# Attention and gated feed-forward on one core: feed-forward steps between the attention's groups, the causal mask of the maxima on VectorE, silu by tanh

## The chip, the cores and the metric

The kernel runs on one core of a Trainium2 chip. The metric is device time in microseconds for one execution, the median of several runs. TensorE (PE) multiplies matrices into PSUM, VectorE (DVE) and ScalarE (ACT) read PSUM, GpSimd (POOL) works on SBUF alone, and SyncE (SP) issues the DMAs. Each engine works off its own instructions in order; semaphores hold one engine until another has done a step.

## What is computed

The input x is 8 x 512 x 128 (batch B, tokens T, channels C), with 16 heads of 8 channels, and all is fp32:

```python
qkv = x @ w_qkv                       # 128 -> 3*128
att = einsum('bhtd,bhsd->bhts', q, k) / sqrt(8)
att = softmax(where(causal, att, -inf))
x = layernorm(x + einsum('bhts,bhsd->bhtd', att, v))
gate, up = x @ (w_gate/127).T, x @ (w_up/127).T      # 128 -> 384
x = layernorm(x + (silu(gate) * up) @ (w_down/127).T)
```

## The kernel before

**Batches and groups.** A batch has 16 heads in four groups of four heads, so there are 32 groups, each named G in the program. `group` on TensorE (line 392 and on) is one step of a software pipeline with five slots. In the step of group G it computes in each slot a part of the scores of G (`scores`, transposed: keys on partitions), two of the ten banks of maxima of group G + 2 (`maxima`), and in slots 1, 2 and 4 the products of the exponentials with V for group G - 1 (`values`). Slot 1 also turns the row maxima of group G + 1 to rows (`turn_negmax`), and in every second group slot 2 turns the attention's output back (`turn_out`). Numbered from a batch's first step, n = 0 also projects V of the next batch and turns x (slot 3), and n = 1 projects Q and K of the batch after the next (slot 3).

**Maxima.** The softmax needs each row's maximum over the causal keys ahead of the scores. `maxima` computes untransposed scores: banks k = 0 to 3 hold 512 keys of one head, banks 4 to 7 hold 384 and 128, banks 8 and 9 hold 256 and 256. Two more bf16 matmuls a bank (`tri`, line 369) add -3e38 to what lies above the diagonal. VectorE's `reduce_group` (line 679) reduces each bank to its maximum by a `tensor_reduce` (line 693). Then POOL splits the maxima in two parts, TensorE turns them, ACT copies them and a DMA puts them into `qx` as two rows more, which the scores' matmuls subtract.

**PSUM.** Eight banks: two pairs (`st_ps`) that scores and projections take in turns, three single banks (`mx_ps`) and one for the values. Place p of a group's sequence uses `mx_ps[p % 3]`. The maxima have the places below, so k = 3 and k = 4 share a bank, the turned maxima lie between k = 4 and k = 5, and the turned output comes before k = 6:

```python
MX_PLACE = (0, 1, 2, 3, 6, 7, 8, 9, 10, 11)
NM_PLACE = 4
OT_PLACE = 5
```

TensorE waits on `mx_reduced` until the bank's reader is done, and with k = 6 of every second group until `attn_made`, which VectorE raises after `normalise` (line 697).

**ACT and POOL.** ACT computes one exponential of 128 x 1024 for each slot (`exp_slot`, line 589) and copies. POOL clears what lies above the diagonal in the exponentials (`clear_diagonal`, line 874), splits the maxima, and adds the attention to x (line 881).

**Feed-forward.** It stands behind all attention, in a loop over the batches (`ffn` on each engine). VectorE makes the statistics (lines 756 and 760), POOL the inverse deviation by a power (line 909) and x1 (line 920), TensorE turns x1, ACT and VectorE split it in a high and a low part, 12 matmuls make gate and up in three pieces of 128 hidden channels (lines 524 and 527), ACT applies silu (line 658), VectorE multiplies (line 791), 24 matmuls go down (line 536), VectorE adds the residual (line 779) and makes new statistics, POOL normalises into `yo` (line 931) and SP stores it.

## Time and profile before

| | us |
|---|---|
| median of three runs | 431.03 (425.5 to 435.24) |
| the profiled execution | 426.48 |
| its span, first to last instruction | 424.8 |
| TensorE busy | 378.4 (89%) |
| VectorE busy | 279.6 (66%) |
| ACT busy | 215.1 (51%) |
| POOL busy | 169.1 (40%) |

The share of busy time is an average over stages. A line of the profile names the engine, the line of the kernel, the operation with output and input, how many were merged, and in brackets how long the engine was idle before and whom it waited for. Ends of matmuls are modelled, and pipelined matmuls overlap, so the distance between two starts says more than a duration. "PEclk" is the granted TensorE clock as a share of 2.4 GHz; 0.5 is the lower level, 1.2 GHz.

### The profile page before, as it was taken

The page shows a single profiled execution, that of the slowest core. Times are in us where ns is not written, and L with a number is a line of the kernel's source. Part 1 is how long each engine was busy: PE and PEld are TensorE (multiplying, and loading weights), DVE is VectorE, ACT ScalarE, POOL GpSimd, SP SyncE. Part 2 cuts the span into 40 slices and gives each one's busy share as a digit, 9 for nine tenths or more (in the row PEclk, how much of TensorE's full clock was granted, in tenths as well). Part 3 has the DMA queues.
Part 4 walks back from the last instruction along what each step waited for, and adds up shares of the span by engine and source line. Part 5 has one row for each costly group of instructions (what it writes and reads, how often), then busy time and mean ns, then how long its engine had stood idle before and what let it go on. Part 6 is the DMA issues. An engine that isn't in the chain of part 4 may idle for free.

```text
span 424.8 us, 8778 instructions
## 1 busy us (share of the span) xinstructions
PE 378.4 (89%) x3285; PEld 223.6 (53%) x3288; DVE 279.6 (66%) x580; ACT 215.1 (51%) x277; POOL 169.1 (40%) x346
## 2 busy tenths in 40 slices
PE   5599979999999999999999999999999886888872
PEld 3344544555555555555555545555555344766761
DVE  6368663745677677768777786777777414777661
ACT  2203553544566666667566675656666564223220
POOL 8701221311423433242243324223432446678844
PEclk9869895955999999999999999999999898999998
DMA  5740562431226425331651443055200000010101
GB/s 167 264 138 3 198 188 66 174 124 41 69 86 217 140 61 200 102 103 56 228 144 55 166 137 102 29 205 164 61 2 5 14 18 0 16 35 25 52 25 49
DMA packets 33897, 41.72 MB, mean 98 GB/s; under 512 B 3136, under 2 KB 17472, under 8 KB 33856
## 3 DMA queue, kind: packets, MB, share of 16 engines
q1 hardware_dynamic: 33856, 41.17, 30.3%
q8 instruction: 26, 0.43, 0.4%
q14 instruction: 15, 0.12, 0.1%
HBM read 21.76 MB, written 18.87 MB: 96 GB/s over the span
## 4 chain that ended last, share of the span: by engine, by line
PE 59%; DVE 21%; POOL 7%; issue 4%; DMA 4%; ACT 3%; SPq 1%; POOLq 0%; DVEq 0%
PE psum L379 16%; PE psum L360 14%; DVE nm L693 13%; PE psum L349 9%; PE psum L325 5%; PE psum L369 4%; POOL x L920 3%; DMA scr_k<-parts 2%; PE psum L389 2%; PE psum L315 2%; PE psum L337 2%; POOL rstd L909 2%; DVE stats L756 2%; PE psum L331 2%; DVE attn L704 1%
## 5 line engine op out<-in xcount | busy, mean ns | idle before, releaser
L693 DVE TENSOR_REDUCE nm<-psum 128x1 f32<-128x512 f32 (+2 forms) x320 | 201.7, 684 | 88.5 <-PE psum L369 88.3
L589 ACT ACTIVATE pt<-psum 128x1024 f32<-128x1024 f32 x160 | 159.6, 1024 | 98.9 <-PE psum L349 98.4
L874 POOL TENSOR_SCALAR_AFFINE_SELECT pt<-pt 128x512 f32<-128x512 f32 x128 | 78.9, 635 | 156.2 <-ACT pt L589 155.9
L360 PE MATMUL psum<-kx,qx 33*128 33x384 f32 (+3 forms) x512 | 101.9, 362 | 15.7 <-DVE nm L693 5.5
L379 PE MATMUL psum<-pt,vx 128*32 128x512 f32 (+3 forms) x1024 | 95.4, 471 | 1.0 <-ACT pt L589 1.0
L349 PE MATMUL psum<-qx,kx 35*128 35x384 f32 (+3 forms) x512 | 84.0, 381 | 2.6 <-DMA qx<-nm_T 1.7
L349 PEld LDWEIGHTS psum<-qx,kx 35*128 35x128 f32 x512 | 44.6, 195 | 68.8 <-issue 51.3
L360 PEld LDWEIGHTS psum<-kx,qx 33*128 33x128 f32 x512 | 60.3, 197 | 31.6 <-DVE nm L693 18.0
L369 PE MATMUL psum<-tri 64*128 64x128 bf16 (+1 forms) x640 | 61.7, 219 | 0.0
L369 PEld LDWEIGHTS psum<-tri 64*128 64x128 bf16 x640 | 29.7, 100 | 23.6 <-issue 20.4
L379 PEld LDWEIGHTS psum<-pt,vx 128*32 128x32 f32 x1024 | 24.3, 111 | 20.4 <-issue 5.4
L658 ACT ACTIVATE sg<-psum 128x512 f32<-128x512 f32 x24 | 14.3, 597 | 28.7 <-PE psum L527 28.7
L881 POOL TENSOR_TENSOR res<-res,attn 128x512 f32<-128x512 f32 x8 | 10.2, 1271 | 41.5 <-DVE attn L704 41.5
L536 PE MATMUL psum<-wT,pt 128*128 128x128 f32 x192 | 22.9, 276 | 1.5 <-DVE pt L791 1.5
L536 PEld LDWEIGHTS psum<-wT,pt 128*128 128x128 f32 x192 | 22.5, 192 | 2.8 <-DVE pt L791 2.3
L527 PE MATMUL psum<-x_lo,wT 128*128 128x512 f32 x48 | 20.5, 426 | 2.0 <-DVE x_lo L772 2.0
L524 PE MATMUL psum<-x_hi,wT 128*128 128x512 f32 x48 | 21.4, 445 | 0.7 <-ACT x_hi L650 0.7
L325 PE MATMUL psum<-xT,wqkv 128*128 128x512 f32 x32 | 20.5, 774 | 0.8 <-ACT xT L568 0.8
L596 ACT ACTIVATE nm_T<-psum 32x128 f32<-32x128 f32 x32 | 8.5, 266 | 22.3 <-PE psum L337 19.6
L862 POOL TENSOR_SCALAR nm_parts<-nm 128x16 fp32r<-128x16 f32 x32 | 6.6, 206 | 28.9 <-DVE nm L695 28.8
L791 DVE TENSOR_TENSOR pt<-psum,sg 128x512 f32<-128x512 f32 x24 | 16.0, 670 | 2.9 <-ACT sg L658 2.0
L672 DVE TENSOR_TENSOR parts<-psum,parts 128x512 fp32r<-128x512 f32 x16 | 11.1, 691 | 9.1 <-ACT parts L575 9.0
(63 smaller groups left out, 289.7 us busy)
## 6 DMA issues: line engine op xcount, KB each, us to landing
scr_q<-parts SPq DMA_DIRECT2D x16, 512.0 KB, 3.2
scr_k<-parts SPq DMA_DIRECT2D x16, 512.0 KB, 4.8
qx<-scr_q SPq DMA_DIRECT2D x64, 128.0 KB, 2.6
kx<-scr_k SPq DMA_DIRECT2D x64, 128.0 KB, 2.7
xa<-L_attn_x SPq DMA_DIRECT2D x8, 256.0 KB, 3.9
res<-L_attn_x SPq DMA_DIRECT2D x8, 256.0 KB, 2.8
out<-yo SPq DMA_DIRECT2D x8, 256.0 KB, 2.2
qx<-nm_T SPq DMA_DIRECT2D x64, 8.0 KB
```

What stands on the lines that cost most here:

```text
L325: pe.matmul(pair[:, n, :], wqkv[:, C * n:C * n + C], xT[:], start=True, stop=True).then_inc((q_made, k_made)[n], 1)
L349: last = pe.matmul(pair[:, bank % 2, col:col + width], kx[u][at:at + KS, 2 * g + hh // 2, P * j:P * j + P].bitcast(F32R), qx[u][at:at + KS ...
L360: pe.matmul(bank[:, col:col + width], qx[u][at:at + KM, 2 * g + hh // 2, P * i:P * i + P].bitcast(F32R), kx[u][at:at + KM, 2 * g + hh // 2 ...
L369: last = pe.matmul(dst, tri[at:at + 64, part, :], mask, start=False, stop=(part == 1), skip_group_check=True)
L379: last = pe.matmul(pv_ps[VW * hh:VW * hh + VW, P * j:T], vx[u][:, at:at + VW], pt[g % 2][:, bank, col:col + T - P * j], start=(j == 0 and ...
L524: pe.matmul(psum[:, bank + k % 2, :], w, x1_hi[u][:].bitcast(F32R), start=True, stop=False)
L527: pe.matmul(psum[:, bank + k % 2, :], w, x1_lo[u][:].bitcast(F32R), start=False, stop=True).then_inc(full, 1)
L536: last = pe.matmul(psum[:, 5, C * n:C * n + C], hid[u][:, m, P * n:P * n + P], wT[:, 2, P * m:P * m + P], start=(m == 0 and n == 0), stop= ...
L589: act.activation(pt[g % 2][:, 2 * s:2 * s + 2, :], next_pair(), ACT.Exp, scale=SM_SCALE).then_inc(exp_done, 1)
L693: dve.tensor_reduce(dst, src, AX.X, ALU.max, negate=True).then_inc(mx_reduced, 1)
L791: dve.tensor_tensor(hid[u][:, m, :], psum[:, 3 + k % 2, :], sg[k % 2][:], ALU.mult).then_inc(hid_made, 1)
L874: pool.affine_select(out=blocks, in_=blocks, pattern=[[0, HG], [1, P]], compare_op=ALU.is_ge, fill=0.0, base=0, channel_multiplier=-1).the ...
```

## The change

- **Order.** A list `RING` names who takes the scores' pairs of PSUM banks, turn by turn, and `side_turns(G)` puts up to two more turns in a group's step, behind slots 1 and 3. A turn "B" is one gate and up piece (4 matmuls), a turn "A" turns x1 of one batch and does the down step of the batch before. The step n = 1 takes the statistics of batch b - 1, n = 2 its turn A (with down of b - 2), n = 3 two turns B of b - 1 and the next n = 0 the third. Only the feed-forward of the last two batches is left for the end.
- **Waits.** `next_pair` waits until the reader of the turn before the last is done (`freed`). For a turn B that is the gating on VectorE (`w_made`) and ACT's copy of up, for a turn A the low part of x1 and the residual (`r2_made`).
- **Mask.** The `tri` matmuls go. VectorE reduces each block of a bank by a `tensor_tensor_reduce` that adds `mask` (fp32, from SBUF) to the block, writes a bf16 copy that nobody reads, and keeps the minimum of the negated sum. That is 16 instead of 10 instructions a group, and in the program each of them is a main instruction and a second one that writes the accumulator to `nm`. The small reduction at line 695 goes. In each place a wait holds a block until the one three before it is done.
- **Silu.** silu(g) = 0.5 g (1 + tanh(g / 2)): ACT computes tanh, VectorE (tanh + 1) * gate, POOL multiplies with a copy of up that ACT made; for the last batch VectorE multiplies from PSUM instead. The factor 0.5 is in the residual's scale.
- **Buffers.** x + attention (`res`) and x1 have two buffers; on SP the load of x into `res` waits for x1 of two batches ago, and the store of a batch's output stands in the loop, four batches behind.

```diff
+def side_turns(G):
+
+
+
+    if G == 0:
+        return None, ("QK", 1)
+    b, n = (G - 1) // NG, (G - 1) % NG
+    if n == 0:
+        return ("B", b - 2, 2) if b > 1 else None, ("VX", b + 1) if b + 1 < B else None
+    if n == 1:
+        return None, ("QK", b + 2) if b + 2 < B else None
+    if n == 2:
+        return None, ("A", b - 1) if b > 0 else None
+    return (("B", b - 1, 0), ("B", b - 1, 1)) if b > 0 else (None, None)
...
+def ring():
+
+    turns = [("X0",), ("QK", 0), ("VX", 0), ("W", 1), ("W", 2)]
+    for G in range(GROUPS + 1):
+        side = side_turns(G)
+        for n in range(SLOTS):
+            if G < GROUPS:
+                turns.append(("S", G, n))
+            if n in (1, 3) and side[n // 2] is not None:
+                turns.append(side[n // 2])
+    return turns + [("B", B - 2, 2), ("A", B - 1), ("B", B - 1, 0), ("B", B - 1, 1), ("B", B - 1, 2), ("A", B)]
+
+
+RING = ring()
...
+            if kind == "A":
+                return ([(x1_lo_made, at[0] + 1)] if at[0] < B else []) + ([(r2_made, at[0])] if at[0] > 0 else [])
+            return [(w_made, HC * at[0] + at[1] + 1)] + ([(up_copied, HC * at[0] + at[1] + 1)] if at[0] < B - 1
+                                                         else [(hid_made, HC * at[0] + at[1] + 1)])
...
-            def next_pair():
-
+            def next_pair(*what):
+
+                assert RING[turn[0]] == what
+                for sem_, value in freed(turn[0]):
+                    pe.wait_ge(sem_, value)
                 turn[0] += 1
                 return st_ps[(turn[0] - 1) % 2]
...
-                diag = [(col + P * i) // P for _, i, col in blocks]
-                diagonal = bank.rearrange("p (m c) -> p m c", c=P)[:, diag[0]:NB:max(1, diag[-1] - diag[0]), :]
-                for part in range(2):
-                    dst = diagonal[:, :, 64 * part:64 * part + 64]
-                    mask = tri[at:at + 64, 2 + part, 0:64 * len(diag)].rearrange("p (m c) -> p m c", c=64)
-                    last = pe.matmul(dst, tri[at:at + 64, part, :], mask, start=False, stop=(part == 1),
-                                     skip_group_check=True)
+                    last = pe.matmul(bank[:, col:col + width],
+                                     qx[u][at:at + KM, 2 * g + hh // 2, P * i:P * i + P].bitcast(F32R),
+                                     kx[u][at:at + KM, 2 * g + hh // 2, 0:width].bitcast(F32R),
+                                     start=(n == 0), stop=(n == len(blocks) - 1), skip_group_check=True)
                 last.then_inc(mx_full, 1)
...
+                elif kind == "A":
+                    if at[0] < B - 1:
+                        turn_x1(at[0], pair[:, 0, :])
+                    if at[0] > 0:
+                        down(at[0] - 1, pair[:, 1, :])
+                    if at[0] == B - 1:
+                        turn_x1(at[0], pair[:, 0, :])
+                else:
+                    gate_up(at[0], at[1], pair)
...
                     if busy:
                         keep_busy(busy)
-                    if s == 3 and X is not None:
-                        pe.wait_ge(exp_done, SLOTS * G + 3)
-                        X(next_pair())
+                    if G >= 0 and s in (1, 3) and side_turns(G)[s // 2] is not None:
+                        side(*side_turns(G)[s // 2])
...
+            def gate_and_up(c, m, pair):
+                act.wait_ge(gate_full, HC * c + m + 1)
+                if c > 0:
+                    act.wait_ge(hid_made, HC * c + m - 2)
+                act.activation(sg[m][:], pair[:, 0, :], ACT.Tanh, scale=0.5 * W_SCALE).then_inc(tanh_done, 1)
+                if c < B - 1:
+                    act.wait_ge(up_full, HC * c + m + 1)
+                    act.activation(us[m][:], pair[:, 1, :], copy).then_inc(up_copied, 1)
...
+            def reduce_bank(M, k):
+                best = nm[M % 2]
+                if k == 0 and M > 1:
+                    dve.wait_ge(nm_split, M - 1)
+                dve.wait_ge(mx_full, MX * M + k + 1)
+                bank = mx_ps[MX_PLACE[k] % 3]
+                blocks = max_blocks(k)
+                for n, (hh, i, col) in enumerate(blocks):
+                    width = P * (i + 1)
+                    count = HG * NB * M + blocks_to(k) + n
+                    if count > 3:
+                        dve.wait_ge(mx_reduced, count - 3)
+                    dve.tensor_tensor_reduce(masked[count % 4][:, 0:width], bank[:, col:col + width],
+                                             mask[:, T - width:T], -1.0, 3.0e38, ALU.add, ALU.min,
+                                             best[:, hh, 3 + i:4 + i]).then_inc(mx_reduced, 1)
...
+                b, n = batch_of(G)
+                if n == 0:
+                    if k == 4 and b > 1:
+                        gated(b - 2, 2)
+                    if k == 5:
+                        normalise(2 * b - 1)
+                elif n == 1:
+                    if k == 3 and b > 0:
+                        stats1(b - 1)
+                    if k == 7 and b + 2 < B:
+                        low_parts(b + 2)
+                elif n == 2:
+                    if k == 5:
+                        normalise(2 * b)
+                    if k == 7 and b > 0:
+                        low_x1(b - 1)
+                    if k == 7 and b > 2:
+                        stats2(b - 3)
+                    if k == 9 and b > 1:
+                        residual2(b - 2)
+                elif k in (4, 8) and b > 0:
+                    gated(b - 1, k // 4 - 1)
+
+            for G in range(-LAG, GROUPS + 1):
+                for k in range(MX):
+                    if G + LAG < GROUPS:
+                        reduce_bank(G + LAG, k)
+                    if G >= 0:
+                        between(G, k)
...
+            def gated(c, m):
+
+                pair = pair_of("B", c, m)
+                dve.wait_ge(tanh_done, HC * c + m + 1)
+                dve.scalar_tensor_tensor(sg[m][:], sg[m][:], 1.0, pair[:, 0, :], ALU.add, ALU.mult).then_inc(w_made, 1)
...
+            def hidden(c, m):
+                pool.wait_ge(w_made, HC * c + m + 1)
+                pool.wait_ge(up_copied, HC * c + m + 1)
+                if c > 0:
+                    pool.wait_ge(y_full, c)
+                pool.tensor_tensor(hid[:, m, :], sg[m][:], us[m][:], ALU.mult).then_inc(hid_made, 1)
+
...
```

The first place is TensorE's step n = 2 of a steady batch, from bank k = 6 on. Before:

```order
L360 MATMUL psum<-kx,qx 128x384 [waits attn_made]
L360 MATMUL psum<-kx,qx 128x128
L369 MATMUL psum<-tri 128x2x64 x2
L360 MATMUL psum<-kx,qx 128x384 [waits mx_reduced]
L360 MATMUL psum<-kx,qx 128x128
L369 MATMUL psum<-tri 128x2x64 x2
L349 MATMUL psum<-qx,kx 128x256 [waits exp_done]
L349 MATMUL psum<-qx,kx 128x256 x3
L360 MATMUL psum<-kx,qx 128x256 [waits mx_reduced]
L360 MATMUL psum<-kx,qx 128x256
L369 MATMUL psum<-tri 128x2x64 x2
```

And now, where L426 are the maxima, L377 turns x1 (`x_1`), L471 is the down step and L414 the scores:

```order
L426 MATMUL psum<-kx,qx 128x384 [waits attn_made]
L426 MATMUL psum<-kx,qx 128x128
L426 MATMUL psum<-kx,qx 128x384 [waits mx_reduced]
L426 MATMUL psum<-kx,qx 128x128
L377 MATMUL psum<-identf,x_1 128x128 [waits x1_lo_made,x1_made,exp_done]
L377 MATMUL psum<-identf,x_1 128x128 x3
L471 MATMUL psum<-wT,hid 128x128 [waits hid_made]
L471 MATMUL psum<-wT,hid 128x128 x11
L414 MATMUL psum<-qx,kx 128x256 [waits exp_done]
L414 MATMUL psum<-qx,kx 128x256 x3
L426 MATMUL psum<-kx,qx 128x256 [waits mx_reduced]
L426 MATMUL psum<-kx,qx 128x256
```

Behind each bank two mask matmuls are gone, and the turn A stands between bank k = 7 and the scores of the last slot: 4 transposes and 12 rows of down, each an fp32 matmul that the trace shows as two (192 for 8 batches).

The second place is TensorE's step n = 3, from the turned maxima (L337, now L399) to bank k = 4. Before:

```order
L337 MATMUL psum<-identf,nm_parts 128x128 [waits nm_split,mx_reduced]
L379 MATMUL psum<-pt,vx 32x512 [waits diag_done,exp_done]
L379 MATMUL psum<-pt,vx 32x512 x3
L349 MATMUL psum<-qx,kx 128x384 [waits exp_done]
L349 MATMUL psum<-qx,kx 128x128
L349 MATMUL psum<-qx,kx 128x384
L349 MATMUL psum<-qx,kx 128x128
L360 MATMUL psum<-kx,qx 128x384 [waits mx_reduced]
L360 MATMUL psum<-kx,qx 128x128
L369 MATMUL psum<-tri 128x2x64 x2
```

Now, where L462 and L465 are gate and up:

```order
L399 MATMUL psum<-identf,nm_parts 128x128 [waits nm_split,mx_reduced]
L439 MATMUL psum<-pt,vx 32x512 [waits diag_done,exp_done]
L439 MATMUL psum<-pt,vx 32x512 x3
L462 MATMUL psum<-x_hi,wT 128x512 [waits x1_hi_made,exp_done]
L465 MATMUL psum<-x_lo,wT 128x512 [waits x1_lo_made]
L462 MATMUL psum<-x_hi,wT 128x512
L465 MATMUL psum<-x_lo,wT 128x512
L414 MATMUL psum<-qx,kx 128x384 [waits exp_done]
L414 MATMUL psum<-qx,kx 128x128
L414 MATMUL psum<-qx,kx 128x384
L414 MATMUL psum<-qx,kx 128x128
L426 MATMUL psum<-kx,qx 128x384 [waits mx_reduced]
L426 MATMUL psum<-kx,qx 128x128
```

The four matmuls of a turn B stand between the values and the scores of slot 2, ahead of bank k = 4.

The third place is VectorE in the step n = 2, a whole group before:

```order
L693 TENSOR_REDUCE nm<-psum 128x1 [waits mx_full,nm_split]
L693 TENSOR_REDUCE nm<-psum 128x1 [waits mx_full] x3
L693 TENSOR_REDUCE nm<-psum 128x4 [waits mx_full] x2
L700 RECIPROCAL rsum<-psum 128x32 [waits o_turned]
L704 TENSOR_TENSOR attn<-psum,rsum 128x4x64 [waits rs_made,res_made]
L693 TENSOR_REDUCE nm<-psum 128x4 [waits mx_full] x2
L693 TENSOR_REDUCE nm<-psum 128x2 [waits mx_full] x2
L695 TENSOR_REDUCE nm<-nm 128x4 [waits mx_reduced]
```

And now its end, from bank k = 7 on, where L682 is the masked reduction with its accumulator's row, `x_lo` the low part of x1, `r_0` the sum before the second norm and L749 the residual:

```order
L682 ISA masked,nm<-psum,mask 128x384 [waits mx_reduced,mx_full]
L682 ISA nm 128x1
L682 ISA masked,nm<-psum,mask 128x128 [waits mx_reduced]
L682 ISA nm 128x1
L731 TENSOR_TENSOR x_lo<-psum,x_hi 128x512 [waits x1_hi_made]
L717 BN_STATS stats<-r_0 128x6 [waits r2_made]
L717 BN_STATS stats<-r_0 128x6 x3
L721 BN_AGGR mv<-stats 128x2 [waits st2_made]
L721 BN_AGGR mv<-stats 128x2 x3
L682 ISA masked,nm<-psum,mask 128x256 [waits mx_reduced,mx_full]
L682 ISA nm 128x1
L682 ISA masked,nm<-psum,mask 128x256 [waits mx_reduced]
L682 ISA nm 128x1
L682 ISA masked,nm<-psum,mask 128x256 [waits mx_reduced,mx_full]
L682 ISA nm 128x1
L682 ISA masked,nm<-psum,mask 128x256 [waits mx_reduced]
L682 ISA nm 128x1
L749 SCALAR_TENSOR_TENSOR r_1<-psum,x_1 128x512 [waits y_full]
```

Each block is two rows now, and the low part of x1, a set of statistics and the residual stand among the last banks.

## Rows read from the trace of the kernel before

**Rows 1.** The page, part 1: busy time and share of the span.
```profile
PE 378.4 (89%) x3285; PEld 223.6 (53%) x3288; DVE 279.6 (66%) x580; ACT 215.1 (51%) x277; POOL 169.1 (40%) x346
```

**Rows 2.** Busy time by stretch: length, then each engine (instructions), granted clock, DMA.
```profile
55.44:108.27 52.83, 50.19 (x369) 26.84 (x365) 28.22 (x51) 24.21 (x31) 12.38 (x25) 0.68 0.41 128
108.27:296.46 188.19, 179.76 (x1821) 103.99 (x1821) 140.38 (x250) 120.65 (x151) 63.23 (x125) 1.00 0.38 124
296.46:349.86 53.40, 49.05 (x506) 26.26 (x509) 31.29 (x63) 33.80 (x41) 21.51 (x43) 0.97 0.08 24
349.86:424.80 74.94, 54.94 (x344) 43.40 (x336) 44.26 (x162) 20.35 (x34) 50.31 (x112) 0.95 0.10 29
```

**Rows 3.** The chain that ended last, in feed-forward: start, length, what.
```profile
373.96 0.67 PE psum L315 x4
...
381.54 0.67 PE psum L315 x4
...
399.31 0.79 DVE stats L756 x4
...
402.49 1.75 POOL x L920 x4
...
407.32 2.69 PE psum L536 x24
```

**Rows 4.** VectorE in order of time: start, length, what, idle time before.
```profile
197.34 2.48 DVE L693 TENSOR_REDUCE nm<-psum 128x1 f32<-128x512 f32 x4
200.88 1.29 DVE L693 TENSOR_REDUCE nm<-psum 128x4 f32<-128x512 f32 x2 [1.07 <-PE psum L369]
...
202.54 0.42 DVE L704 TENSOR_TENSOR attn<-psum,rsum 128x256 f32<-128x256 f32 x1
203.68 2.48 DVE L693 TENSOR_REDUCE nm<-psum 128x4 f32<-128x512 f32 x4 [0.72 <-PE psum L369]
...
223.56 1.29 DVE L693 TENSOR_REDUCE nm<-psum 128x2 f32<-128x512 f32 x2 [1.05 <-PE psum L369]
```

**Rows 5.** TensorE in order of time, the same group and the next.
```profile
198.68 0.33 PE L337 MATMUL psum<-identf,nm_parts 128*128 128x128 f32 x1
198.94 1.06 PE L379 MATMUL psum<-pt,vx 128*32 128x512 f32 x8
199.93 0.51 PE L349 MATMUL psum<-qx,kx 35*128 35x384 f32 x4
200.27 0.51 PE L360 MATMUL psum<-kx,qx 33*128 33x384 f32 x4
...
209.93 0.33 PE L369 MATMUL psum<-tri 64*128 64x128 bf16 x4
210.19 0.85 PE L379 MATMUL psum<-pt,vx 128*32 128x384 f32 x8
```

**Rows 6.** Groups of instructions by form: busy, mean ns of one, idle before.
```profile
L658 ACT ACTIVATE sg<-psum 128x512 f32<-128x512 f32 x24 | 14.3, 597 | 28.7 <-PE psum L527 28.7
...
L693 DVE TENSOR_REDUCE nm<-psum 128x1 f32<-128x512 f32 x128 | 79.6, 683 | 21.1 <-PE psum L369 21.0
...
L881 POOL TENSOR_TENSOR res<-res,attn 128x512 f32<-128x512 f32 x8 | 10.2, 1271 | 41.5 <-DVE attn L704 41.5
...
L760 DVE BATCH_NORM_AGGREGATE mv<-stats 128x2 f32<-128x6 f32 x64 | 6.1, 157 | 2.3
...
L779 DVE SCALAR_TENSOR_TENSOR r<-psum,x 128x512 f32<-128x512 f32 x8 | 5.5, 692 | 12.3 <-PE psum L536 12.3
...
L658 ACT ACT_TABLE_LOAD x1 | 1.3, 1283 | 0.0
```

**Rows 7.** All engines in order of time, feed-forward.
```profile
410.31 0.39 PE L524 MATMUL psum<-x_hi,wT 128*128 128x512 f32 x1
...
410.54 0.39 PE L527 MATMUL psum<-x_lo,wT 128*128 128x512 f32 x1
...
411.78 0.38 DVE L760 BATCH_NORM_AGGREGATE mv<-stats 128x2 f32<-128x6 f32 x4
```

632 lines of the change are left out of this document (269 added, 363 removed).

## Prediction

> **What bounds the kernel now.** I read the page first: TensorE is busy for 378.4 of 424.8 us, far above every other engine [rows 1]. That average hides four stretches, so I cut the span at the projections of V that mark batch borders [rows 2]. In the first (batch 0 to 1) the granted clock is 0.68, so mostly the lower of the two levels, and TensorE is busy for 50.19 of 52.83 us. The next five batches run at the upper level, 188.19 / 5 = 37.64 us each. Then come 53.40 us of the last attention and 74.94 us of feed-forward, where TensorE is busy 54.94 us and no engine is full. There the chain repeats every 381.54 - 373.96 = 7.58 us [rows 3]: a chain of latencies, not work.
>
> Inside a steady batch I read VectorE in order of time [rows 4]. Four 512-wide reductions take 2.48 us, one alone 0.683 [rows 6], so one costs (2.48 - 0.683) / 3 = 0.599 us back to back: 512 elements at the 0.96 GHz that this gives are 0.533, and 0.064 is fixed (0.597 in all from here on). Then comes an idle 1.07 us in every group, and, in every second one, 0.72 us behind `attn`. They are not waits for a busy TensorE only. Bank k=4 lies in the same PSUM bank as k=3, so TensorE may fill it only when k=3 is read; and k=6 waits for `attn_made`. The reader sees a ring of three banks that makes VectorE and TensorE take turns: the group is a chain through both. From the first reduction to k=4 it is 200.88 - 197.34 = 3.54 us; on TensorE this is the transpose of the maxima at 198.68, values at 198.94, scores at 199.93, maxima at 200.27 [rows 5].
>
> **The change, part by part.** *Mask off TensorE.* 640 matmuls go, 20 in each group. Four take 210.19 - 209.93 = 0.26 us of its queue [rows 5]: 1.3 us a group, 5.2 a batch. On the chain only those between a bank's maxima and its reduction count, about 0.15 us at four places.
>
> *Mask on VectorE.* 10 reductions a group become 16 masked ones, each with an accumulator read behind it: 32 instructions. The elements stay 5120, so 5.33 us. The masked operation isn't in this trace. Its nearest row is the SCALAR_TENSOR_TENSOR from PSUM, 692 ns for 512 [rows 6], 0.159 over its elements, as the reduction has 0.150, so I take 0.064 back to back. The read is nearest to BATCH_NORM_AGGREGATE: four in 0.38 us, 157 ns alone, so (0.38 - 0.157) / 3 = 0.074 each [rows 6, 7]. I take 0.065, as it is one element. Then a block costs its elements + 0.129, a group 5.33 + 16 x 0.129 = 7.4 us where it was 10 x 0.597 = 6.0. Bounds: 0.064 if the read hid entirely, 0.314 if both showed their full 157 ns.
>
> The Trainium skill, in "VectorE: DVE Perf Modes", section "The TRN2 errata", gives 120 fixed cycles to an operation that reads PSUM and 58 to one that reads SBUF; by it a block would cost 0.125 + 0.06 = 0.185 us over its elements (an estimate). The 0.064 us of the row is half of that for a PSUM source, and I go by the row. Its price is a rival below.
>
> *Feed-forward between the groups.* For each batch TensorE gets 12 gate/up matmuls at 410.54 - 410.31 = 0.23 us, 24 down matmuls in 2.69 and four transposes in 0.6: 6.0 us [rows 3, 7]. VectorE gets three gatings, x1's low part and the residual at 0.6 each and two sets of statistics of 1.3 us (0.79 and 0.38 with the gap between [rows 3, 7]): 5.6 us. ACT gets eight operations of 0.6 us [rows 6], 4.8 us on 120.65 / 5 = 24 of 37.64, POOL 3 x 1.27 for the products (as L881 [rows 6]) and two norms; both have room. SP's new waits, x1 of two batches ago and the store of four batches ago, are for things about a batch old; queued behind them are a load of x and the maxima's rows, which the scores wait for, but nothing is held.
>
> So a batch asks TensorE for about 37.6 - 2.8 of waits - 5.2 + 6.0 = 35.6 us and VectorE for 4 x 7.4 + 3 of normalising and low parts + 5.6 = 38.2. VectorE becomes the busier engine, and the handoffs remain.
>
> *The steady batch, group by group on VectorE*, from first reduction to first reduction (k0-3 take 2.64 us, each later bank 0.79). Second group (with QK): statistics of 1.3 us fill the gap before k=4, k=7 ends at 7.1, the low parts wait for ACT until 8.5, then two banks: 10.1 us. Third group: k=4 at 3.5 (3.54 less a mask, plus the slower k=1), `attn` at 5.9, k=6 at 6.4, k=7 done 8.0. TensorE meanwhile turns x1 and does the 24 down matmuls, 6.3 to 9.6, and only then scores and k=8, which starts at 10.4; k=9 ends at 12.0, the residual at 12.6, and the next group's scores wait for it, since they take its pair: 0.9 more, 13.5 us. Fourth group: gate/up in front of the scores puts k=4 at 4.45, two gatings add 1.2: 10.7. First group: the same k=4, one gating, normalising, 0.5 behind `attn` and 0.7 behind the V turn (1.05 now [rows 4]): 11.8. Sum **46.1 us** a batch, where it is 37.64.
>
> *Sum.* Up to the V projection of batch 1: 108.3 - 4 (masks at low clock, gain between 0 and 7) = 104.3. Batch 1 has no down step: 42.8. Batches 2 to 5: 184.4. Batch 6 has no QK: 44.7. To the start of the last group 18.5 (2.5 + 6.5 + 9.5, no maxima any more). That is 394.7. The end is a new chain: values and two gate/up turns 3.6, tanh and gating 1.3, then three runs from statistics to a norm at 404.24 - 399.31 = 4.93 us each [rows 3] with products and attention sum (3 x 1.27) between, down twice 5.5, transposes, x1's parts and gate/up 2.7, the first tanh 0.6, six VectorE products 3.7, residual 0.7, store 2.2, handoffs 2.5: 41.5 us. It replaces the 74.94. Total 436 of span against 424.8, and with the 1.7 us around it 438 against the profiled run's 426.5. The runs of before have a median of 431.0 (425.5 to 435.2); I keep 438, as the profiled run is one of this kind and its offset can fall either way.
>
> Against before: 4 and 33.4 us are saved at the two ends; the batches 1 to 5 cost 227.2 instead of 188.2, and from there to the last group 63.2 instead of 53.4. Net 11 us more.
>
> **Rivals.** *The stalls don't add up* (20%): if TensorE gets ahead wherever VectorE is behind, the batch is VectorE's 38.2 plus half of the 8 us of idle time, 42 us: 438 - 4.1 x 6.7 = 411, faster. For it: TensorE has 35.6 only. Against: `attn_made`, k=3 before k=4 and the pairs of the ring are hard waits, and 37.64 - 140.38 / 5 = 9.6 us of idle VectorE a batch are there today [rows 2]. It decides if a batch stays below 43.5 us.
>
> *The masked reduction is dearer* (22%): each 0.01 us over 0.129 costs 0.64 us a batch, some 4.6 us in all. If the read can start only when the main operation has ended, a block costs 0.157 + 0.065 = 0.222 over its elements: 438 + 43 = 481. With both latencies open it is 520, and half way to the first, 0.175, it is 459. For it: no row shows two instructions tied in this way. Against: all plain pairs of VectorE in the trace overlap by 0.09 us. By the page's fixed terms above, 0.185, the time would be 464 (an estimate).
>
> *TensorE's clock falls* (10%): it would be busy for 77% of a batch where it is 95% now; in the feed-forward stretch, at 73%, the granted clock is 0.95 [rows 2], so the risk is small. The first stretch shows the price, 52.83 - 37.64 = 15 us for a batch; one or two such make 453 to 468.
>
> *The change as worked out* (48%): 425 to 452.
>
> Silu by tanh costs one product more per piece; its gain is that no table has to be loaded between exponentials. The trace shows a load of 1.28 us before the first silu [rows 6]. 
>
> **How the numbers follow.** A measurement of this kernel tells 2% from no change: 422.4 and 439.6. The likeliest case lies on both sides of the upper bound: 0.29 same, 0.19 slower. Rival one: 0.18 faster, 0.02 same. The dearer reduction: 0.22 slower. The clock: 0.09 slower, 0.01 same. Together faster 0.18, same 0.32, slower 0.50. The range leaves out the fastest fifth of rival one and the far end of the dear reduction: 408 to 474. The likeliest case alone: 425 to 452.
>
> **What would show it.** Right: steady batches of 44 to 48 us with VectorE busy over 80%; masked 512-wide operations near 690 ns with reads that add 65; k=4 some 4.4 us after k=0 in groups with gate/up; first scores behind the down step late by `r2`; some 41 us after the last group begins. Wrong: batches near 42 (rival one), reads that start only when the main operation has ended (rival two), a clock below 0.9 after batch 1 (rival three).

## The result, and the profile after

The changed kernel takes **481.3 us** in the median of 4 runs (477.76 to 485.47), the kernel before 433.13 beside it (4 runs). The ratio is 1.121, 95% interval 1.095 to 1.147: slower by 12%, and 7 us above the upper end of the range. (Ratios and their intervals here compare the undisturbed runs of both kernels, taken beside each other on one chip; medians are over all runs.) The profiled execution took 485.47 us, its span is 483.7 and its mean granted clock 0.794, where it was 0.932.

From the page of the changed kernel: part 1, the clock in 40 slices of 12.1 us each (part 2), the two groups of the masked maxima (part 5):

```profile
PE 412.5 (85%) x2648; PEld 227.4 (47%) x2648; DVE 299.1 (62%) x1255; ACT 224.6 (46%) x297; POOL 189.9 (39%) x346
...
PEclk9897598566579968995897799987885589679576
...
L682 DVE CUSTOM_DVE_ANT_0 masked<-psum,mask 128x384 bf16<-128x384 f32 (+3 forms) x512 | 220.3, 487 | 118.9 <-PE psum L426 105.9
...
L682 DVE DVE_READ_ACCUMULATOR2_ANT nm<- 128x1 f32 x512 | 42.6, 83 | 0.0
```

TensorE issues 637 matmuls fewer than in [rows 1] and is busy 34 us longer. That is the first thing to see: work went away, busy time rose. A matmul at the lower clock level takes twice as long (the 24 of a down step 5.46 us in the rows at the end, 2.69 in [rows 3]), and the digits of the clock fall to 5 to 8 again and again in the middle of the run, where [rows 2] has 1.00 for 188 us.

Busy time by stretch, cut at the projections of V as in [rows 2]; the clock is the third number from the right. (The projections stand at 255.59 and 358.09; the cuts at 255.90 and 358.90 lie a little behind them.)

```profile
54.20:100.07 45.87, 43.85 (x286) 22.94 (x285) 30.14 (x134) 24.48 (x31) 11.62 (x24) 0.72 0.39 123
100.07:153.56 53.49, 49.91 (x302) 25.91 (x300) 33.87 (x146) 28.58 (x38) 18.48 (x35) 0.71 0.29 93
...
204.57:255.90 51.33, 45.73 (x330) 26.13 (x327) 35.72 (x156) 27.75 (x37) 22.99 (x43) 0.87 0.30 96
...
358.90:420.00 61.10, 55.63 (x357) 30.06 (x359) 37.83 (x175) 29.75 (x39) 27.09 (x49) 0.70 0.04 11
420.00:483.70 63.70, 35.74 (x224) 24.25 (x216) 16.86 (x58) 14.95 (x21) 27.79 (x53) 0.71 0.09 25
```

The four batches from 153.56 to 358.09 take 204.5 us, 51.0 to 51.5 each, all at 0.87. Against the sum on record: 100.07 where 104.3 was forecast (-4.2); 53.5 for 42.8 (+10.7); 204.5 for 184.4 (+20.1); 125.6 for 104.7 (+20.9). Together 47.5 us over a span of 436.

Inside one of these batches, TensorE's waits, and the same batch cut where the clock changes (`r` is the sum before the second norm, `sg` the gated product, `nm` the maxima):

```profile
209.17 0.50 PE L426 MATMUL psum<-kx,qx 33*128 33x512 f32 x1 [0.29 <-DVE nm L682]
234.39 0.50 PE L414 MATMUL psum<-qx,kx 35*128 35x512 f32 x2 [1.46 <-DVE r L749]
235.98 0.49 PE L426 MATMUL psum<-kx,qx 33*128 33x512 f32 x1 [0.42 <-DVE nm L682]
242.82 0.51 PE L414 MATMUL psum<-qx,kx 35*128 35x384 f32 x4 [0.67 <-DVE sg L738]
246.91 0.50 PE L414 MATMUL psum<-qx,kx 35*128 35x512 f32 x2 [0.72 <-issue]
248.50 0.50 PE L426 MATMUL psum<-kx,qx 33*128 33x512 f32 x1 [0.42 <-DVE nm L682]
255.16 0.51 PE L426 MATMUL psum<-kx,qx 33*128 33x384 f32 x4 [0.91 <-DVE attn L694]
```

```profile
204.57:220.00 15.43, 14.75 (x122) 7.88 (x122) 13.99 (x65) 11.03 (x15) 10.00 (x19) 1.00 0.16 48
220.00:230.00 10.00, 10.00 (x54) 6.68 (x47) 5.66 (x25) 2.68 (x4) 2.45 (x5) 0.50 0.57 211
230.00:237.00 7.00, 5.00 (x49) 3.46 (x52) 4.22 (x18) 3.00 (x4) 1.06 (x3) 0.99 0.00 1
237.00:240.00 3.00, 3.00 (x11) 1.18 (x6) 0.76 (x4) 0.34 (x2) 0.64 (x1) 0.50 0.14 36
240.00:255.90 15.90, 12.98 (x105) 6.94 (x104) 11.09 (x46) 10.71 (x15) 8.84 (x16) 0.99 0.41 123
```

Most of the waits are ones the prediction speaks of: scores behind `r`, scores behind the gating `sg`, a bank behind `attn`. (For the one of 0.72 us the profile names no releaser; by `RING` the scores there also wait for `sg`, whose gating ends at 246.81.) The three of 0.29 and 0.42 us are not: there bank k = 3 waits until the reduction of k = 0 is done, since both use the same PSUM bank. All seven add up to 4.9 us in the batch. In the kernel before the longest such wait in a steady batch is 0.31 us:

```profile
127.73 0.51 PE L360 MATMUL psum<-kx,qx 33*128 33x384 f32 x4 [0.31 <-DVE attn L704]
```

What was not in the sum is the low clock: 10 us and then 3 us at the lower level, with TensorE busy all the time. The 3 us come right behind the waits of 1.46 and 0.42 us. The 10 us do not: in the 14 us ahead of 220 TensorE stands still for 0.7 us in all, 0.29 of them in one wait, and in the 15.43 us before the fall it is busy for 96%. In the batches from 153.56 and from 307.06 both falls come at the same places; in the one from 255.59 the long one comes 10 us earlier.

So there are two readings. **Theory A**: TensorE's short waits let its clock fall, and the low clock is the loss. **Theory B**: the handoffs of the ring and VectorE's longer turns are the loss by themselves, and the clock is an accompaniment. Where an experiment gives TensorE matmuls of zeros, they read a tile of zeros that the kernel has for its start.

### The profile page after: what moved, and what is told of

The parts are those of the page before. It is cut to its first block and busy times, and to the rows that moved or that the text cites. A ratio compares the mean times of both kernels' runs of the same rounds, so it can differ in the third digit from the quotient of the medians.

```text
span 483.7 us, 8440 instructions
## 1 busy us (share of the span) xinstructions
PE 412.5 (85%) x2648; PEld 227.4 (47%) x2648; DVE 299.1 (62%) x1255; ACT 224.6 (46%) x297; POOL 189.9 (39%) x346
## 5 line engine op out<-in xcount | busy, mean ns | idle before, releaser
L682 DVE CUSTOM_DVE_ANT_0 masked<-psum,mask 128x384 bf16<-128x384 f32 (+3 forms) x512 | 220.3, 487 | 118.9 <-PE psum L426 105.9
L439 PE MATMUL psum<-pt,vx 128*32 128x512 f32 (+3 forms) x1024 | 116.9, 560 | 0.3 <-ACT pt L593 0.3
L426 PE MATMUL psum<-kx,qx 33*128 33x384 f32 (+3 forms) x512 | 102.8, 378 | 16.8 <-DVE nm L682 8.5
L414 PE MATMUL psum<-qx,kx 35*128 35x384 f32 (+3 forms) x512 | 91.6, 412 | 16.9 <-DVE r L749 7.3
L414 PEld LDWEIGHTS psum<-qx,kx 35*128 35x128 f32 x512 | 50.6, 223 | 97.5 <-issue 69.4
L426 PEld LDWEIGHTS psum<-kx,qx 33*128 33x128 f32 x512 | 60.7, 221 | 44.0 <-DVE nm L682 31.5
L471 PE MATMUL psum<-wT,hid 128*128 128x128 f32 x192 | 33.3, 352 | 16.4 <-POOL hid L895 14.7
L682 DVE DVE_READ_ACCUMULATOR2_ANT nm<- 128x1 f32 x512 | 42.6, 83 | 0.0
L471 PEld LDWEIGHTS psum<-wT,hid 128*128 128x128 f32 x192 | 32.6, 267 | 17.3 <-issue 15.1
L895 POOL TENSOR_TENSOR hid<-sg,us 128x512 f32<-128x512 f32 x21 | 26.9, 1279 | 2.4 <-DVE sg L738 2.4
L462 PE MATMUL psum<-x_hi,wT 128*128 128x512 f32 x48 | 24.1, 503 | 1.8 <-DVE hid L743 1.1
L465 PE MATMUL psum<-x_lo,wT 128*128 128x512 f32 x48 | 20.8, 433 | 0.2 <-DVE x_lo L731 0.2
L462 PEld LDWEIGHTS psum<-x_hi,wT 128*128 128x128 f32 x48 | 10.5, 218 | 21.1 <-issue 17.4
L738 DVE SCALAR_TENSOR_TENSOR sg<-sg,psum 128x512 f32<-128x512 f32 x24 | 16.3, 680 | 4.5 <-ACT sg L617 4.5
```

The source lines that it names most:

```text
L414: last = pe.matmul(pair[:, bank % 2, col:col + width], kx[u][at:at + KS, 2 * g + hh // 2, P * j:P * j + P].bitcast(F32R), qx[u][at:at + KS ...
L426: last = pe.matmul(bank[:, col:col + width], qx[u][at:at + KM, 2 * g + hh // 2, P * i:P * i + P].bitcast(F32R), kx[u][at:at + KM, 2 * g + ...
L439: last = pe.matmul(pv_ps[VW * hh:VW * hh + VW, P * j:T], vx[u][:, at:at + VW], pt[g % 2][:, bank, col:col + T - P * j], start=(j == 0 and ...
L462: pe.matmul(pair[:, n, :], w, x1_hi[:].bitcast(F32R), start=True, stop=False)
L465: pe.matmul(pair[:, n, :], w, x1_lo[:].bitcast(F32R), start=False, stop=True).then_inc(full, 1)
L471: last = pe.matmul(dst[:, C * n:C * n + C], hid[:, m, P * n:P * n + P], wT[:, 2, P * m:P * m + P], start=(m == 0 and n == 0), stop=(m == H ...
```

## The experiments

**1. The mask back on TensorE.** In the changed kernel, the turns of the feed-forward stay:

```diff
+    last = pe.matmul(dst, tri[at:at + 64, part, :], mask, start=False, stop=(part == 1),
+                     skip_group_check=True)
...
-    dve.tensor_tensor_reduce(masked[count % 4][:, 0:width], bank[:, col:col + width],
...
+    dve.tensor_reduce(dst, src, AX.X, ALU.max, negate=True).then_inc(mx_reduced, 1)
```

> The changed kernel with the mask of the maxima back on TensorE (20 mask matmuls a group, 10 plain reductions on VectorE); feed-forward still in turns. Theory A (the granted TensorE clock falls because TensorE pauses, and that costs some 45 us): the mask matmuls fill pauses, the mean clock rises from 0.80 to 0.87 or more, and the time comes to 450 to 465 us. Theory B (the waits of the new turns alone make the time, and the clock only follows): VectorE's part of the chain is nearly as long (6.0 instead of 6.6 us a group) and TensorE has 1.3 us more a group, so 475 to 490 us.

456.75 us (450.82 to 464.16), ratio 1.058 (1.039 to 1.077), mean clock 0.864. The batches take 47.93, 54.13 and 48.92 us at clocks of 0.96, 0.78 and 0.93. The turns alone make the kernel slower, and the batch's length goes with its clock, as theory A had it.

**2. Only the mask moved.** The kernel before with the masked maxima on VectorE; feed-forward at the end, silu as before:

```diff
-    dve.tensor_reduce(dst, src, AX.X, ALU.max, negate=True).then_inc(mx_reduced, 1)
...
+    dve.tensor_tensor_reduce(masked[count % 4][:, 0:width], bank[:, col:col + width],
+                             mask[:, T - width:T], -1.0, 3.0e38, ALU.add, ALU.min,
+                             best[:, hh, 3 + i:4 + i]).then_inc(mx_reduced, 1)
```

> The kernel before with one part of the change, the causal mask of the maxima on VectorE; feed-forward at the end, silu as before. Theory A: TensorE has 5 us less work in 37.6, pauses more, and the granted clock falls below 1.00 in the steady batches (1.00 before): 440 to 460 us. Theory B: the chain of a group is as long as before (2.45 instead of 2.40 us for the first four banks), the first batches gain up to 5 us: 420 to 432 us, with clock 0.93 as before.

475.15 us (457.15 to 497.82; before, beside it, 432.81), above the 440 to 460 of theory A and far above theory B's 420 to 432. The profiled run is the fastest one, 457.15 us at a mean clock of 0.801. Three of its stretches:

```profile
96.16:134.53 38.37, 35.23 (x287) 19.02 (x285) 30.15 (x134) 24.71 (x31) 11.90 (x25) 0.95 0.35 116
134.53:177.86 43.33, 41.33 (x287) 21.13 (x284) 30.15 (x134) 23.80 (x31) 13.75 (x27) 0.77 0.40 125
...
261.22:309.57 48.35, 47.60 (x286) 24.89 (x284) 30.15 (x134) 24.36 (x31) 12.78 (x26) 0.64 0.30 99
```

The same instructions, VectorE busy 30.15 us in each, and 38.4 to 48.4 us: of what the rows show only the clock differs. TensorE's longest waits here are 0.35 to 0.55 us. Neither part of the change is harmless by itself.

**3. Zeros where TensorE waits.** In the changed kernel, matmuls of zeros ahead of its waits. They add nothing to the result (they accumulate zero into the tile of the values, or write zeros into it where it is free):

```diff
+def fill(n, start=False):
+    for _ in range(n):
+        pe.matmul(pv_ps, zeros[:, 0:P], zeros[:], start=start, stop=False,
+                  skip_group_check=True)
...
+    if G > 1 and s == 0 and n == 3:
+        fill(5)
+    if G > 1 and s == 3 and n == 3:
+        fill(3)
...
+    fill(3)
     pe.wait_ge(attn_made, OT + 2)
...
+    if k == 3 and G > 0:
+        if n % 2 == 0:
+            pe.wait_ge(ot_copied, 2 * b + n // 2 + 1)
+        fill(2, start=(n % 2 == 0))
```

So five stand ahead of the scores that wait for `r`, three ahead of those that wait for `sg` and of the bank that waits for `attn`, two ahead of the fourth bank.

> The changed kernel with matmuls by zeros (bf16, 512 columns, added to the values' bank or written to it when it is free) in the places where TensorE waits: two ahead of bank k=3, three ahead of k=6 behind the turned output, five and three ahead of two scores in the step n=3. They change no result. Theory A: the granted clock rises from 0.80 to above 0.90 and the time falls to 435 to 455 us although TensorE has 400 matmuls more. Theory B: the fillers lengthen TensorE's own way where it is not waiting, 480 to 495 us.

441.74 us (438.24 to 444.31), ratio 1.031 (1.018 to 1.044), mean clock 0.923. Stretches, and one of the filled waits:

```profile
187.12:232.95 45.83, 44.43 (x350) 23.74 (x346) 35.45 (x155) 27.66 (x37) 22.68 (x43) 1.00 0.32 103
...
324.68:390.00 65.32, 62.49 (x445) 31.89 (x441) 39.03 (x179) 35.61 (x45) 32.95 (x61) 0.82 0.08 23
```

```profile
211.82 1.25 PE L453 MATMUL psum<-zeros 128*128 128x512 bf16 x5
213.35 0.50 PE L414 MATMUL psum<-qx,kx 35*128 35x512 f32 x2 [0.28 <-DVE r L763]
```

More work on TensorE, 39.6 us less time. A batch goes from 51.1 to 45.8 us with the same turns, the same VectorE operations (35.45 us) and the clock at 1.00. That is theory A's forecast; by B this kernel had to be slower than the changed one.

**4. The residual two banks earlier**, so that the next scores wait less for `r`:

```diff
-    if k == 9 and b > 1:
+    if k == 7 and b > 1:
         residual2(b - 2)
```

> The changed kernel with one instruction of VectorE moved: the residual of the step n=2 stands ahead of bank k=8 instead of behind k=9, so the next group's first scores needn't wait for it (1.46 us a batch in the trace). Theory A: that pause is one of those before a fall of the clock, so the time falls by more than the pause, 15 to 30 us, to 450 to 467. Theory B: it falls by the pause alone, 6 x 1.5 = 9 us, to 472.

463.5 us (459.95 to 472.67), ratio 1.080 (1.064 to 1.096), clock 0.823. Some 18 us for a wait that is worth 1.5 us in a batch by itself: two of its batches have 0.89 and take 47.9 us, two others 0.82 and 0.80 and take 50.0 and 51.2. Its batch from 99.21 to 141.11 has no down step yet and is the changed kernel's code unaltered. It ran at 1.00 in 41.90 us; the changed kernel took 53.49 for it at 0.71.

**5. Zeros and the early residual together.** To experiment 3:

```diff
     if G > 1 and s == 0 and n == 3:
-        fill(5)
+        fill(1)
...
-    if k == 9 and b > 1:
+    if k == 7 and b > 1:
```

> The changed kernel with the zero matmuls of e3_fill and, as in e4_residual_early, the residual of the feed-forward taken before the last two banks of its group; in front of the last group's scores one zero matmul is left of five. If TensorE's clock is what costs (theory A), the clock in the steady batches stays at 0.97 or more, as in e3_fill, and a batch loses the 1.5 us of the late residual against the 45.8 us of e3_fill: 44 to 45 us, in all 430 to 435 us. If the clock falls at that one place where fillers went from five to one, batches come back to 47 to 51 us and the time to 450 to 460. If the time is made by the waits of the turns alone (theory B), e4_residual_early already showed all of the gain, and this kernel is at 460.

436.64 us (428.54 to 438.3; before, beside it, 432.76), clock 0.915. The batches of 1.00 take 44.68 us, 1.15 less than in experiment 3, as expected; two others came to 0.89 and 0.93 and the last two stretches to 0.81 and 0.79, so the total is above the 430 to 435. The fastest run, 428.54, is within 1% of the fastest of the kernel before beside it, 425.72.

**6. A pause in the kernel before.** This is the direct test: nothing of the change, only a wait. Three memsets of an unused tile on VectorE, once in each of six batches, and TensorE waits for them ahead of the next group's first scores:

```diff
+    if n == 2 and 0 < b < 7:
+        for m in range(3):
...
+            dve.memset(idle[:, m, :], 0.0).then_inc(paused, 1)
...
+    if G % NG == 0 and 4 < G < 30:
+        pe.wait_ge(paused, 3 * (G // NG - 1))
```

> The kernel before, with one pause a batch in batches 1 to 6: after the reductions of the third group VectorE sets three unused 128x512 tiles to zero (about 0.55 us each, 1.6 to 1.8 us together), and TensorE waits for them before it takes up the last group's scores; nothing else is changed. If a pause costs only itself (theory B), six pauses add 10 to 12 us: 442 to 446, with the clock at 1.00 in the steady batches. If a pause also lowers the clock behind it (theory A), the granted clock of the steady batches is below 0.95, a batch grows by more than 3.5 us, and the time is 455 or more.

494.88 us (483.55 to 517.07; before, beside it, 432.76, 425.72 to 501.7): 62 us for six pauses of 2.0 to 2.1 us, and still 58 from the fastest run to the fastest. The pause in TensorE's order of time (slowest of these runs), and the batch around it:

```profile
232.08 0.79 PE L351 MATMUL psum<-qx,kx 35*128 35x512 f32 x2 [2.11 <-issue]
```

```profile
220.00:230.00 10.00, 9.41 (x105) 5.55 (x97) 8.11 (x16) 6.23 (x8) 3.56 (x7) 1.00 0.44 161
230.00:232.00 2.00, 0.00 (x0) 0.00 (x0) 1.81 (x5) 0.00 (x0) 0.43 (x2) 0.94 0.67 250
232.00:256.05 24.05, 23.97 (x146) 12.62 (x146) 10.81 (x19) 10.04 (x12) 4.76 (x8) 0.50 0.31 89
```

Full clock before this pause, half behind it, for the rest of the batch and beyond. The five paused batches take 48.5 to 56.0 us where they took 37.64. Theory B expected 442 to 446.

**7. Zeros in experiment 2**, ahead of the fourth and the seventh bank (in the same way as above):

```diff
+    if k == 3 and PV is not None and G <= 32:
...
+        fill(2, start=(n_ % 2 == 0))
...
+    if k == 6 and OT is not None and G <= 32:
+        fill(3)
```

> e2_mask_only (the kernel before with the causal mask of the maxima on VectorE and nothing else, 475.15 us) with zero matmuls on TensorE where it waits in a group: two of 128x512 before the fourth bank, three before the seventh. If the clock makes e2_mask_only slow (theory A), the clock rises to 0.97 or more in the steady batches, which come to 38 to 41 us each, and the time to 425 to 440. If VectorE's longer reductions make it slow (theory B), the fillers bring nothing: 470 to 480.

**412.34 us** (410.81 to 417.55), ratio 0.959 (0.946 to 0.972), 63 us less than experiment 2 (46 from the fastest run to the fastest) and faster than both kernels:

```profile
55.97:96.08 40.11, 39.40 (x302) 19.41 (x298) 30.15 (x134) 24.06 (x30) 11.55 (x24) 0.91 0.40 128
96.08:133.18 37.10, 36.39 (x302) 18.36 (x298) 30.14 (x134) 24.07 (x30) 12.84 (x26) 1.00 0.42 137
...
336.00:409.60 73.60, 53.91 (x324) 42.72 (x322) 44.43 (x162) 19.76 (x33) 48.92 (x109) 0.95 0.10 30
```

Five batches of 37.1 us against 188.19 for five save 2.8 us, the stretch at the start saves 12.7 ([rows 2] has 52.83), and the end is unchanged. It came out better than the 425 to 440 expected: I had given VectorE's longer reductions up to 3 us a batch, and at full clock they are hidden.

**8. Zeros at the start of the kernel before**: those of experiment 7 in the first nine groups only (`G <= 8`), and seven more where TensorE waits for a transfer:

```diff
+    if G == 2 and s == 0:
+        fill(7)
     if s == 0:
         pe.wait_ge(nm_loaded, NM_LOADED * G + NM_LOADED)
```

> The kernel before, with zero matmuls only in its first nine groups: seven before the scores of the third group, where TensorE waits for a transfer, two before the fourth bank and three before the seventh in each group. Its first stretch ran at a granted clock of 0.68. If the pauses at its start are what lowered it (theory A), the stretch of batch 0 to 1 gets a clock over 0.85 and loses 5 to 12 us of its 52.8: 419 to 428. If the low clock there has another cause, the zero matmuls only take up time: 433 to 440.

424.63 us (415.63 to 457.62), ratio 0.969 (0.951 to 0.987). The stretch from 55.63 to 96.39 has a clock of 1.00 and takes 40.76 us, 12.1 less than in [rows 2]. The kernel before had lost this to the low clock, and zeros ahead of its waits bring it back; which of the filled waits mattered, the run doesn't tell.

The profile (432.79 us) shows one thing more. Behind the ninth group it is the kernel before, unaltered, and two neighbouring batches read:

```profile
210.20:247.82 37.62, 35.92 (x368) 20.79 (x364) 28.09 (x50) 24.05 (x31) 12.84 (x26) 1.00 0.37 122
247.82:293.87 46.05, 45.22 (x367) 25.20 (x364) 28.09 (x50) 24.44 (x31) 14.24 (x27) 0.75 0.37 117
```

The clock falls at 270.4, where the last wait of TensorE was one of 0.31 us, and stays at the lower level for 51 us of unbroken work. A batch can thus lose 8.4 us with no wait that its neighbours don't have.

**9. The pause of experiment 6, filled:**

```diff
     if G % NG == 0 and 4 < G < 30:
+        fill(9)
         pe.wait_ge(paused, 3 * (G // NG - 1))
```

> e6_pause (494.88 us) with nine zero matmuls of 128x512 on TensorE in front of each of its six waits, so that VectorE's three memsets and the wait stay, but TensorE works through the 2.1 us. If TensorE's pause lowers the clock (theory A), the steady batches return to a clock of 1.00 and to 37.6 + 2.1 = 39.7 us each: 438 to 446. If the late start of the group, or VectorE's extra work, is what costs, it stays above 480.

437.82 us (434.75 to 444.73), ratio 1.003 (0.990 to 1.016). VectorE's memsets and the late start of the group are all still there:

```profile
146.31:186.09 39.78, 38.05 (x378) 21.59 (x374) 29.54 (x53) 24.06 (x31) 12.81 (x26) 1.00 0.40 131
186.09:227.41 41.32, 39.65 (x377) 21.98 (x374) 29.53 (x53) 24.03 (x31) 12.80 (x26) 0.96 0.33 108
```

39.78 is 37.64 + 2.14: with TensorE at work through it, the delay costs itself and no more. So it is TensorE's standing still, not the lateness, that costs the rest. It isn't what starts every fall: in the two batches of 41.32 us (0.96) the clock still falls, 0.3 and 1.0 us ahead of the zeros, and two of the falls of experiment 6 begin 0.4 us ahead of their pause, at the same place of the group. But there the clock stayed low for 27 us or more each time, here for 3.4.

**10. One pause in place of six:**

```diff
-    if G % NG == 0 and 4 < G < 30:
-        pe.wait_ge(paused, 3 * (G // NG - 1))
+    if G == 12:
+        pe.wait_ge(paused, 3)
```

> The kernel before with one pause of about 2.1 us in place of six: TensorE waits for the three memsets at the first group of batch 3 only. By the first run with six, (494.88 - 432.8) / 6 = 10.3 us each, of which 2.1 are the wait. If the clock falls behind a single pause and comes back by itself (theory A), this kernel's clock is 0.50 for a stretch of 15 to 40 us behind the pause and 1.00 after it, and the time 441 to 452 us. If only repeated pauses lower the clock, it is 433 to 436.

441.4 us (436.03 to 485.1), ratio 1.002 (0.992 to 1.012). The kernel before was itself at 445.07 (433.69 to 496.59) beside it, so the total tells little. The stretches do:

```profile
108.07:145.71 37.64, 35.96 (x367) 20.79 (x365) 28.08 (x50) 24.47 (x31) 12.11 (x26) 1.00 0.35 111
145.71:170.00 24.29, 21.54 (x221) 12.85 (x218) 18.66 (x34) 14.38 (x19) 9.45 (x19) 0.97 0.42 143
170.00:172.00 2.00, 1.81 (x11) 1.15 (x11) 0.47 (x2) 0.98 (x1) 0.00 (x0) 0.50 0.00 0
172.00:190.00 18.00, 18.00 (x114) 9.23 (x111) 8.45 (x15) 7.90 (x11) 2.92 (x6) 0.50 0.23 69
190.00:192.00 2.00, 2.00 (x16) 0.92 (x12) 1.80 (x4) 0.43 (x1) 0.00 (x0) 0.50 0.70 221
192.00:193.51 1.51, 1.51 (x21) 0.80 (x13) 0.18 (x1) 0.35 (x1) 1.18 (x1) 0.81 0.95 286
193.51:231.14 37.63, 35.93 (x367) 20.79 (x364) 28.08 (x50) 24.47 (x31) 12.15 (x26) 1.00 0.33 108
```

With one pause of 2.12 us, from 168.07 to 170.19, this batch takes 47.80 us, 10.2 more than its neighbours. The clock is at 0.50 from 168.7, within the pause, to about 192.6 (the last 1.51 us have a mean of 0.81), then comes back by itself. This is one batch of one trace, and the unpaused batch of experiment 8 lost 8.4 us; the weight lies on experiments 6 and 9, with five paused batches each.

**11. Experiment 7 with the seven matmuls of zeros of experiment 8 at the start:**

```diff
+    if G == 2 and s == 0:
+        fill(7)
```

> e7_mask_fill (412.34 us) with the seven zero matmuls of e8_before_fill in front of the third group's scores, where TensorE waits for the first transfer. In e7_mask_fill the clock was 0.91 in the stretch at 55.97 to 96.08 us, 40.1 us long where the later ones are 37.1. If the pause at that transfer causes it, the stretch comes to 37 or 38 us: 405 to 410. If it doesn't, 411 to 415.

424.53 us (420.11 to 429.94), ratio 0.971 (0.959 to 0.984). Half right. The stretch from 55.84 takes 38.71 us at 1.00, as the pause at the transfer no longer comes ahead of it. But a later batch ran at 0.92 (40.16 us) and the stretch from 283.02 to 340 at 0.68, with no wait of TensorE over 0.35 us in it; experiment 7's trace has the same waits there and 0.97. I can't name what makes the difference. The intervals of the ratios of 7 and 11 overlap, so the two versions are not told apart.

**12. Experiment 1 with the zeros and the early residual of experiment 5**: what the turns alone cost with the clock held.

```diff
+    if G > 1 and s == 0 and n == 3:
+        fill(1)
...
-    if k == 9 and b > 1:
+    if k == 7 and b > 1:
```

> e1_mask_on_pe (the feed-forward in turns, the mask still on TensorE, 456.75 us) with the zero matmuls of e5_fill_early and its earlier residual. It shows what the turns alone cost once the clock holds. By the chain of the forecast, with VectorE's plain reductions (6.0 us a group in place of 7.4) and the mask matmuls back on TensorE (5.2 us a batch), a batch is 43 to 46 us at a clock of 1.00, and the time 425 to 440; e5_fill_early has 44.7 us a batch with the mask on VectorE. If the turns' batch is bound by VectorE and not by the chain through both engines, it is 41 or less.

444.19 us (442.7 to 445.88), ratio 1.020 (1.012 to 1.028):

```profile
194.57:241.21 46.64, 46.05 (x427) 26.83 (x423) 33.62 (x71) 27.81 (x37) 22.78 (x43) 1.00 0.33 107
...
334.46:390.00 55.54, 53.51 (x503) 30.11 (x501) 36.13 (x82) 32.91 (x43) 29.20 (x53) 0.97 0.08 23
```

46.6 us a batch, just above the 43 to 46 expected, as the time is above the 425 to 440, with VectorE busy 33.6. The turns' batch isn't bound by VectorE. TensorE is busy for 46.05 us of it, zeros included: here the fillers take room themselves, and the turns with the mask's matmuls leave little.

At a clock of 1.00 a steady batch is thus:

| kernel | us a batch |
| --- | --- |
| before | 37.64 |
| mask on VectorE, zeros (7) | 37.1 |
| turns, mask on TensorE, zeros, early residual (12) | 46.6 |
| the whole change, zeros (3) | 45.8 |
| the whole change, zeros, early residual (5) | 44.7 |

## Why the prediction failed

**The step that failed** is the third rival, "TensorE's clock falls". It had 10% and a price of one or two batches at low clock, because TensorE would be busy for 77% of a batch and the clock is 0.95 in the feed-forward stretch at 73% [rows 2], "so the risk is small". Both halves are wrong. First, busy share did not foretell the clock. TensorE is busy for 45.73 of 51.33 us in the changed kernel, 89% (more than the forecast 77% partly because its matmuls take longer at the low clock), and 96% in the 15 us ahead of the first fall. Experiment 6 has 94% in its five paused batches and a clock of 0.62 to 0.75. What the runs show in its place: the changed kernel spends 13 to 14 us of each steady batch at the lower level, that costs 5 us a batch and some 40 in all, and zeros in the places of the waits give it back (481.3 to 441.7, experiment 3). So the waits bring the low clock on the whole. What starts a single fall stays open: the longer one of each batch has no wait over 0.29 us in the 14 us ahead of it in three of the four batches, and experiments 8 and 11 have falls with no new wait at all. Second, the comparison was with the wrong row. Why the feed-forward stretch keeps 0.95 with longer waits than these no run here settles, but it says nothing on a dense stretch with short ones. The warning was in the first row of the same group: 52.83 us at 0.68, TensorE 95% busy. I took that clock as a property of the start and never asked what TensorE had done before it. Experiment 8 asked, and won 12.1 us in the kernel before.

The Trainium skill describes such a case, in "TensorE: Matmul & The Clock Gate", section "A second HAM failure mode: psum-queue depth-cycling": a kernel that turned in a few PSUM banks idled briefly between groups of matmuls, and its clock went up and down between the two levels. The trace here agrees in that: 1.00, 0.50, 0.99, 0.50 and 0.99 in one batch of the ring.

The second rival named 481 us, and 481.3 was measured. That is luck: its mechanism, a block at 0.222 us over its elements, did not come (0.08 below).

**By the steps of the sum:**

- *To the projection at 108.3: 104.3 forecast, 100.07 came.* The masks' end at low clock was given 4 us, bounds 0 and 7; 8.2 came, and the clock was 0.72 where it had been 0.68.
- *The batch without a down step: 42.8 forecast.* The same code at a clock of 1.00 took 41.90 us (experiment 4). So of the 10.7 us too much, the clock makes 11.6 and the chain -0.9.
- *Batches 2 to 5: 46.1 each forecast; 51.1 came, and 45.8 once the clock held* (experiment 3). The clock accounts for the 20.1 us. The agreement of 46.1 and 45.8 is partly luck, see the next point.
- *A masked block costs its elements + 0.129.* Too much. 512-wide operations start 0.61 us apart (235.23 and 235.84 below), so a block is its elements + 0.08 (128 wide, at 241.87 and 242.08, it is 0.21, the same 0.08 over): the read (83 ns) starts together with the next operation and is nearly hidden, 0.61 against the 0.597 of a plain reduction. A group is 5.33 + 16 x 0.08 = 6.6 us, not 7.4, and with every block on the chain a batch would be 46.1 - 64 x 0.049 = 43.0 (an estimate). Of the 2.8 us from there to 45.8 the zeros take some; how much stays open. The mechanism on record, that the read can start only behind its operation, is refuted:

```profile
235.23 0.69 DVE L682 CUSTOM_DVE_ANT_0 masked<-psum,mask 128x512 bf16<-128x512 f32 x1 [0.98 <-POOL nm_parts L836]
235.84 0.08 DVE L682 DVE_READ_ACCUMULATOR2_ANT nm<- 128x1 f32 x1
235.84 0.69 DVE L682 CUSTOM_DVE_ANT_0 masked<-psum,mask 128x512 bf16<-128x512 f32 x1
```

- *Bank k=4 some 4.4 us behind k=0 in a group with gate/up.* At full clock it is 218.74 - 214.18 = 4.56 us (experiment 3); at low clock 241.39 - 235.23 = 6.16. The chain was read correctly.
- *The scores behind the down step wait 0.9 us for `r`.* 1.46 here. Right in place, short in size, and one of the short falls of the clock comes right behind it.
- *The tail of 41.5 us from the last group.* From 434.45 (below) to 483.7 it is 49.3. The two down steps take 5.46 us each at the lower level where 2.69 was forecast, in all 5.5 more, and TensorE stands 14.68 us for the last products on GpSimd just before the first. Some 2.3 us are left, which I put down to my handoffs; no run shows it.

```profile
434.45 1.06 PE L439 MATMUL psum<-pt,vx 128*32 128x512 f32 x8 [0.34 <-ACT pt L593]
...
456.38 5.46 PE L471 MATMUL psum<-wT,hid 128*128 128x128 f32 x24 [14.68 <-POOL hid L895]
...
469.86 5.46 PE L471 MATMUL psum<-wT,hid 128*128 128x128 f32 x24 [1.75 <-DVE hid L743]
```

- *The rest between:* 76.4 us from 358.09 to the last group for 63.2 forecast, at a clock of 0.71. Experiment 12 needs 109.6 us from its last projection of V to the end, where the clock is 0.97 and then 0.82; 104.7 was forecast. So of the 20.9 us too much some 16 go with the clock; the other 5 are between the clock that is still low there, that kernel's own mask matmuls and what I had too low, and I can't part them.
- *TensorE's own work in a batch, 37.6 - 2.8 of waits.* [rows 2] has (188.19 - 179.76) / 5 = 1.7 us of idle time, so the sum is 36.7 us and not 35.6. *VectorE busy over 80%* was a sign of being right; it is 35.72 of 51.33 us, 70%, and 35.45 of 45.83, 77%, with the clock held.
- *Silu by tanh, one table load:* as forecast, one load, the products 1.28 us each.

**What was right:** the change is slower; a ring of banks turns overlapping work into a chain; the feed-forward in turns costs the steady batches more than it gives back at the end. With the clock held most of the time the whole change is still 3.1% slower (experiment 3), and its 441.7 us lies within the likeliest case's own 425 to 452; with the residual earlier as well (experiment 5) no difference from the kernel before is shown. "The stalls don't add up" is refuted, since no batch with a down step is below 44 us in any kernel with the turns, at full clock too. The likeliest case described the kernel as it would be with a steady clock; the kernel doesn't have one.
